# Scores of cached and new keys in one pass, with the keys of the pair three later turned behind a pair's projection

## The reference

```python
q = rope(rmsnorm(x @ Wq.T, q_norm_w), pos)        # 32 query heads of 128
k = rope(rmsnorm(x @ Wk.T, k_norm_w), pos)        # 8 key heads
v = x @ Wv.T
kc, vc = k_cache[block_table], v_cache[block_table]    # 512 cached keys of each row
k_all, v_all = concatenate([kc, k]), concatenate([vc, v])   # 512 + 32 keys of a row
scores = where(valid, q @ k_all.T * SCALE, -1e30)
o = softmax(scores) @ v_all
x = x + o @ Wo.T
```

## Time and profile before

| what | value |
|---|---|
| times of three runs | 1452.36, 1454.44 and 1454.81 us, median 1454.44 |
| span of the profiled execution | 1451.3 us |
| TensorE busy | 1356.5 us, 93% of the span |
| VectorE busy | 1132.6 us, 78% |
| GpSimd busy | 973.1 us, 67% |
| ScalarE busy | 766.9 us, 53% |
| bytes moved | 188.72 MB, 130 GB/s |

### The profile page before, as it was taken

One profiled execution on the slowest core, in us unless ns is written; L12 is line 12 of the kernel. 1 busy time (PEld: TensorE's weight loads), 2 busy tenths in 40 slices (PEclk: granted clock), 3 DMA queues, 4 the chain that ended last, 5 costly groups with the idle time before them and its releaser, 6 DMA issues.

```text
span 1451.3 us, 28498 instructions
## 1 busy us (share of the span) xinstructions
PE 1356.5 (93%) x8640; PEld 1162.0 (80%) x8640; DVE 1132.6 (78%) x2891; ACT 766.9 (53%) x1989; POOL 973.1 (67%) x1269
## 2 busy tenths in 40 slices
PE   2599999998999999999999999999999999999889
PEld 1478888887878888887777888888787888888777
DVE  6688877777887778788877878887888888777754
ACT  1356555555664555556554555666555556555431
POOL 5676777777766677776766777777777777676500
PEclk8699999999999999999999999999999999999999
DMA  6434444454543343436533433445544343435401
GB/s 228 133 87 121 133 119 134 123 173 133 173 117 116 125 119 125 135 108 202 164 117 107 138 112 112 128 125 181 170 142 129 104 129 117 131 122 167 124 22 58
DMA packets 61380, 188.72 MB, mean 130 GB/s; under 512 B 10736, under 2 KB 11504, under 8 KB 58608
## 3 DMA queue, kind: packets, MB, share of 16 engines
q0 software_dynamic: 40960, 134.25, 31.3%
q1 hardware_dynamic: 19504, 53.50, 10.5%
q10 hardware_dynamic: 864, 0.46, 0.1%
HBM read 177.95 MB, written 12.32 MB: 131 GB/s over the span
## 4 chain that ended last, share of the span: by engine, by line
PE 69%; DVE 21%; issue 5%; ACT 2%; DMA 1%; DVEq 1%; POOL 0%; SPq 0%; ACTq 0%; POOLq 0%
PE PROJ L182 13%; PE MISC L182 13%; PE O L359 10%; PE S L182 10%; PE PT L349 8%; PE KT L338 5%; DVE probs L736 4%; PE O L361 3%; DVE scores L729 2%; PE PROJ L328 2%; DVE kT_lo L750 2%; DVE rope_v L703 2%; PE PROJ L330 2%; DVE mask L716 2%; DVE rope_u L699 2%
## 5 line engine op out<-in xcount | busy, mean ns | idle before, releaser
L976 POOL DMA_INDIRECT kv_rows<-in_kv,step_idx x512 | 529.8, 1035 | 219.6 <-issue 117.8
L550 ACT ACTIVATE pT<-PT 128x640 f32<-128x640 f32 x256 | 180.2, 704 | 300.6 <-PE PT L349 300.6
L359 PEld LDWEIGHTS O<-pT,kv_rows 128*128 128x128 f32 x2048 | 262.6, 192 | 27.0 <-ACT pT L550 9.8
L359 PE MATMUL O<-pT,kv_rows 128*128 128x128 f32 x2048 | 274.8, 277 | 2.9 <-ACT pT L550 2.6
L546 ACT ACTIVATE kT_hi<-KT 128x512 fp32r<-128x512 f32 x256 | 151.2, 590 | 225.1 <-PE KT L338 225.0
L750 DVE TENSOR_TENSOR kT_lo<-KT,kT_hi 128x512 fp32r<-128x512 f32 x256 | 176.0, 687 | 71.3 <-ACT kT_hi L546 70.7
L554 ACT ACTIVATE probs<-scores,min_all 128x640 f32<-128x640 f32 x256 | 212.7, 831 | 23.3 <-DVE min_all L729 21.0
L349 PEld LDWEIGHTS PT<-ident,probs 128*128 128x128 f32 x1280 | 142.1, 141 | 89.9 <-DVE probs L736 78.7
L349 PE MATMUL PT<-ident,probs 128*128 128x128 f32 x1280 | 191.3, 280 | 22.7 <-DVE probs L736 22.3
L729 DVE CUSTOM_DVE_ANT_0 scores<-S,mask,min_new 128x512 f32<-128x512 f32 x256 | 190.5, 744 | 0.0
L182 PE MATMUL PROJ<-w_hi,x_hi 128*128 128x512 f32 x384 | 172.0, 448 | 15.0 <-DVE w_lo L663 12.6
(11 more groups left out here) (215 smaller groups left out, 2702.6 us busy)
## 6 DMA issues: line engine op xcount, KB each, us to landing
stage<-in_wqkv SPq DMA_DIRECT2D x12, 1024.0 KB, 7.7
x_raw<-in_xT SPq DMA_DIRECT2D x32, 256.0 KB, 4.2
stage<-in_wo SPq DMA_DIRECT2D x8, 1024.0 KB, 6.6
kv_rows<-in_kv,step_idx POOLq DMA_INDIRECT x512, 3.7
y_tile<-y_running SPq DMA_DIRECT2D x32, 256.0 KB, 3.7
y_running<-y_tile SPq DMA_DIRECT2D x31, 256.0 KB, 2.1
out<-kv_rows SPq DMA_DIRECT2D x8, 256.0 KB, 2.0
stage<-in_w1T SPq DMA_DIRECT2D x1, 1024.0 KB, 6.7
```

Source lines behind the costliest of these rows:

```text
L359: nc.tensor.matmul(O[:, 0:P], kv_rows[:, b, c, GK * D + h * D:GK * D + (h + 1) * D], pT[:, c * P:(c + 1) * P], start=c == 0, stop=False)
L550: nc.scalar.activation(pT[:, :], PT[:, 0:KEYS], ACT.Copy).then_inc(sm["pT_ready"], 1)
L976: G.indirect_dma_start(kv_rows[:, b, c, :], None, kv[:, :], bass.IndirectOffsetOnAxis(ap=step_idx[:, b * LC + c:b * LC + c + 1], axis=0)). ...
```

## The change

**Scores.** The new keys are no longer scored apart. Each pair's high and low key parts lie in one of 4 slots (`kT`, 544 columns: 512 cached keys and the 32 new ones, which VectorE's `fill_slots` copies twice a tile for 4 slots each). `score` makes 544 columns in two pieces of 288 and 256, six products in all, into one two-bank buffer SX. `new_scores`, its minima, the 32-column copy and the masks made on VectorE are gone; the masks are made once, go to DRAM, and are loaded for two rows at a time. The minimum is one operation over 544 columns.

**Order.** TensorE's step p is now: `turn_probs` of pair p, `score` of pair p + 2, the chunks of the projection, `turn_keys` of pair p + 3, `weigh` of pair p. All 4 chunks of block 0 stand in step 0, block 1's in steps 1 and 2, block 2's in steps 3 and 4. `turn_q` of head 0 stands in step 4, `turn_k` in step 5, `turn_q` of head 1 in step 6. Two chunks of `project_out` stand ahead of the last `weigh`, six behind it. Every tile of the loop is written out or looped by the same `walk`.

```diff
-                score(i, 0)
-                turn_kv(i, 1)
-                project_some(0)
-                for p in range(PAIRS - 1):
-                    score(i, p + 1)
-                    turn_probs(i, p)
-                    if p + 2 < PAIRS:
-                        turn_kv(i, p + 2)
-                    elif not last:
-                        turn_kv(i + 1, 0)
-                    project_some(p + 1)
...
+                fill = [[(0, c) for c in range(KC)], [(1, 0), (1, 1)], [(1, 2), (1, 3)],
+                        [(2, 0), (2, 1)], [(2, 2), (2, 3)], [], [], []]
+
+                for p in range(PAIRS):
+                    turn_probs(i, p)
+                    if p + 2 < PAIRS:
+                        score(i, p + 2)
+                    elif not last:
+                        score(i + 1, p + 2 - PAIRS)
+                    for k, c in fill[p] if not last else []:
+                        proj(i + 1, k, (c, 1), wcount)
+                    if not last and p == 4:
+                        pe.wait_ge(sm["y_added"], CREDIT + i)
+                        turn_q(i + 1, 0)
+                    if not last and p == 5:
+                        turn_k(i + 1)
+                    if not last and p == 6:
+                        turn_q(i + 1, 1)
+                    if p + 3 < PAIRS:
+                        turn_keys(i, p + 3)
+                    elif not last:
+                        turn_keys(i + 1, p + 3 - PAIRS)
+                    if p == PAIRS - 1:
+                        project_out(i, 0, (0, REP // 2), g * HALVES + WO_FIRST + 2)
+                    weigh(i, p)
```

**VectorE** in step p: `normalise` of pair p + 1, `minimum` of p + 2, the rotation in steps 1, 2 and 4, `rest_kT` of pair p + 3, then `take_o`:

```diff
+                for p in range(PAIRS):
+                    if p + 1 < PAIRS:
+                        normalise(i, p + 1)
...
+                    if not last:
+                        if p in (1, 2, 4):
+                            rotate(i + 1, p // 2)
+                        if p == 5:
+                            rest_qT(i + 1, 0)
+                            rest_kT_new(i + 1)
+                            fill_slots(i + 1, 0)
+                    if p + 3 < PAIRS:
+                        rest_kT(i, p + 3)
```

**GpSimd** has the table of the tile after next between the last rotation and the gathers of rows 1 and 2, and the values are copied four times with all but one row's tokens multiplied by 0 (one product of 128x1024 instead of a copy of 128x256):

```diff
+                for k in range(2):
+                    make_rstd(i + 1, k)
+                    rotate_sum(i + 1, k)
...
+                take_indices(tn, 0, ROWS - 1, 2 * i + 3)
+                next_values(0)
+                make_rstd(i + 1, 2)
+                rotate_sum(i + 1, 2)
+                if not (final and fixed and t == TILES - 2):
+                    make_table(i + 2, (t + 2) % TILES if fixed else t + 2)
+                next_values(1)
+                next_values(2)
```

More of the change, by code:

```diff
@@ new lines, in body @@
+                if not final and fixed and t == TILES - 2:
+                    next_half(g + 1, 4)
+                if fixed and t == 0:
+                    if final:
+                        load_l1(0)
+                        load_l1(1)
+                    else:
+                        next_half(g + 1, 0)
+                        next_half(g + 1, 1)
+                if last:
+                    for b in range(ROWS):
+                        n = 1 if b == ROWS - 1 else 2
+                        sp.wait_ge(sm["pv_done"], CREDIT + i * PAIRS + b // 2 * GK + GK)
+                        sp.dma_start(y_all[:, 2 * b:2 * b + n, :], y_rows[2 * b:2 * b + n, :, :].rearrange("t p n -> p t n")
+                                     ).then_inc(l1_y_in[b], 16)
@@ new lines, in rest_weights @@
+            def rest_weights(g, t, p, final):
+                for m in range(HALVES):
+                    own = m >= WO_FIRST
+                    if (t, p) != LO_AT[m] or (final and not own):
+                        continue
+                    hi, lo = half_parts(m)
+                    rest_half((g if own else g + 1) * HALVES, m, lo, hi, stage[:, m % 2, :, :])
+                for m in range(4):
+                    if final and (t, p) == L1_LO_AT[m]:
+                        hi, lo = l1_parts(m)
+                        rest_half(GROUPS * HALVES, m, lo, hi, l1_stage(m))
@@ L891, in body @@
-                if not last:
-                    take_new_scores(i + 1)
                 add_y(i, y_all[:, TILES - 1, :] if last else y_tile[:, :])
```

874 lines of the change are left out of this document (442 added, 432 removed).

## The result

The changed kernel took **1732.68 us** (median of 4 runs, 1728.04 to 1737.15) against 1454.62 us of the kernel before: 1.192 times as long, interval 1.189 to 1.194. A later run beside its own runs of the kernel before gave 1.193 (1.189 to 1.197). The forecast was 1666 us with a range of 1512 to 1719: the sign and most of the size are right, and the time lies 14 us above the range.

What follows compares the result with a forecast made beforehand. TensorE was taken to bound the kernel. From 1451.3 us, 31 tiles at 7.0 more gave +217, boundaries and ends −33, so 1635; 1638 as a median with the clock held, plus 28 for the clock: 1666 us, range 1512 to 1719.

Steps and rivals of the forecast that it cites:

- the joint pass removes work of TensorE: Scoring new keys with cached ones removes 1.8 us a tile and adds 0.6: TensorE's work falls from 39.0 to 37.8.
- the score waits for a remainder behind a rotation: Steps 3 and 5: TensorE's score waits about 1.9 us each for the keys' remainder, which stands behind VectorE's rotation; bounds 0 and 2.5.
- row 1's keys set the tile: Block 2, rotation, table, then row 1's gathers: next tile's row 1 keys there at 40.6 us, period 47.4, 7.0 more.
- what TensorE waits in its last steps: Steps 6 and 7, without projection: TensorE's step 3.0 us against VectorE's 3.9, so 0.9 us more each (0.4 to 1.5).
- the price of the clock: Half-speed TensorE behind row 1's wait: 0.9 us a tile, the shorter price in six tiles of ten, 28 us in all.
- the piece behind row 1's keys: End of each tile, from turning row 1's keys: 0.36, two chunks 1.48, weighing 1.03, six chunks 4.28; 7.15 us.
- the two prices of the earlier trace: Half of TensorE's half-clock stretches behind waits of 2.46 and 3.54 us: 1.5 and 2.6 us.
- the step from 47.8 to 47.4: Tile period of 47.8 us taken as 47.4, since the table's products follow one another a little faster than they last.
- The rule of the Trainium skill: A TensorE standing still for data each round can be slowed each round; for all tiles that gives 1684 to 1719 us.
- group boundaries: Four places where groups end and begin, costing 41.7 us before: 20 us less (bounds 0 and 41).
- start and end: First wait for gathered keys 8 us less (0 to 18.75); last tile, without projection, 5 us less (0 to 10).

Runs made afterwards that it cites:

- g4: Changed kernel in the shallow order, keys and queries turned ahead of the chunks, table between row 1's and row 2's gathers; 1386.5 us, 0.954 of the kernel before.
- e4: Changed kernel with scores one pair ahead, keys two, table behind row 1's gathers, one output chunk ahead of the last weighing; 1427.7 us, 0.984 of the kernel before.
- e1: Changed kernel with the next table made behind all gathers instead of ahead of row 1's gathers; 1619.8 us, 1.115 of the kernel before.
- e2: Changed kernel with 8 needless TensorE products per tile just ahead of its wait for row 1's keys; 1682.1 us, 1.158 of the kernel before.
- e5: e1 with 6 needless TensorE products per tile ahead of its wait for row 1's keys; 1636.7 us, 1.118 of the kernel before.
- f2: Same kernel as g4, on the second kind of chip: f3 with the table between row 1's and row 2's gathers; 1465.7 us, 0.992 of the kernel before.
- f3: Changed kernel in the tuned shallow order, eight gathers of rows 1 and 2 in a row, table behind them; 1615.1 us, 1.092 of the kernel before.

## Why the prediction was right in kind and too low in size

How the 284 us between the spans divide can be worked out from the two traces. Where the granted clock was 0.50, half of TensorE's busy time is taken as lost; that is an estimate. In the kernel before it is 13.8 of 1356.5 us busy, in the changed one 107.2 of 1403.6. So the work at full clock fell from 1342.7 to 1296.4 us, by 46; the clock's share grew by 93; and idle time grew from 94.8 to 331.7, by 237. −46 + 93 + 237 = 284. The same working gives 1290.4 us of work for g4 and 1298.1 for e4, which have the same 8896 products in another order.

1. **Right: the joint pass removes work of TensorE.** It was put at 1.2 us a tile, some 37 us; by the working above it is about 46.
2. **Right: the score waits for a remainder behind a rotation**, 1.51 us where 1.9 was worked out, twice in a tile.
3. **Right: row 1's keys set the tile**, by the chain that was named: 40.62 us on the mean for 40.6. That it fits to 0.1 us is in part luck: the squares of block 2 ended 0.5 us sooner than worked out, and from there to the turned keys it took 14.2 us for 13.8. e1 shows that the place of the table decides.
4. **Right: what TensorE waits in its last steps.** Two waits of 0.9 us were worked out for the last pairs, 1.8 together, and 0.67 and 1.35 came (661.59 and 666.50), 2.0 together. They lie ahead of row 1's wait and cost no time of their own while that stands, other than by the clock.
5. **Wrong: the price of the clock**, the step that failed. The sum took 0.9 us a tile: the shorter price of the earlier trace rows, 1.5 us, in six of ten tiles. The clock fell in each of the 20 tiles away from group boundaries, and the piece behind row 1's keys took 9.31 us on the mean for the sum's 7.15: 2.16 us a tile, between the two prices of the earlier trace rows. e2 gives 2.1 of it back. Over 31 tiles that is 67 us for the 28 of the forecast, 39 too few. The other 12 of the 51 us that the tiles are short come from the step from 47.8 to 47.4, for table products that follow one another faster than they last: 40.62 + 7.15 is 47.8. Taking "six of ten" from the length of row 1's wait alone was the error. Three other waits lie just ahead of it. e1 has the clock fall behind 1.20 us with them, where the earlier trace rows had it hold behind 1.97, and in e5, with the last wait filled, the three others alone let it hold. The rule of the Trainium skill that the prediction set beside its sum ("TensorE: Matmul & The Clock Gate", "HAM oscillation — how this bites in real kernels") names the case that came: paid in each round.
6. **Wrong: group boundaries.** They were to cost 20 us less than the 41.7 of before. The three tiles around the first took 52.7, 53.7 and 58.0 us, and the loop's 1595.2 less 31 ordinary tiles of 49.93 leaves 47, some 8 of it in the first tile: 26 us more than forecast. The halves of the weights stand in the same chains of ScalarE and VectorE that TensorE now waits for, but no run took this apart, and the cause is open.
7. **Right: start and end**, 16.5 us less for 13.

The forecast has the tiles (49.93 − 48.3) × 31 = 51 us too low, the boundaries 26 too low and the ends 3.5 too high: 73, which is, but for rounding, the 72 us between the span of 1735.3 and the forecast's 1662.9 for it.

## What to carry to other kernels

When work is taken out of the engine that bounds, look at what its last operands wait for before the order is made deeper: here a table of eight small products, 2.2 us on an engine with slack, stood ahead of a gather and cost 113 us, and the deeper order itself still cost 4% beside the shallow one once both had their feeders in order. Price a wait of TensorE that comes in every tile with the clock that it loses in every tile, and count the waits just ahead of it too: here 2.2 us on the mean, where the trace of before had 1.5 and 2.6. And compare kernels on one chip, since some chips add waits of their own; there, part long rows of gathers with other work.

## What the runs showed of the hardware that was not expected

- Needless products can pay: 248 products of 128x512 in waits made the kernel 51 us faster (e2).
- The granted clock depends on more than the wait behind which it falls: with the same waits to 0.06 us it held in one tile and fell in the next (e1). With the last of these waits filled it held at 1.00 in each of 20 tiles (e5).
- Two kinds of chips show up. On those where the kernel before takes 1453 to 1455 us, ScalarE has 9 to 12 us of waits without a releaser in a whole run, with eight gathers in a row or not. On those where it takes 1464 to 1476 us, it has 53 to 118 with at most six in a row and 151 to 263 with eight; 2.2 us of other work between the fourth and the fifth took 149 us off 1615 on one of them (f2, f3).
- Chips differ by more than the kernel before shows: that took 1453 to 1476 us, 1.6% apart, and one shallow order 1427.7 and 1526.3 us, 6.9% apart.
